# The FFN norm's variance kept spread over the features, the Newton step of queries and keys on GpSimd, and another slot order

## What is computed

```python
# attention, 16 heads of 64, windows of 32 tokens with one window of look-back
q, k, v = split(shift_tokens(x) @ Wqkv)
q = l2norm(q) * qs;  k = l2norm(k) * ksc      # then rotary tables
x = softmax(q k^T * 8, masked) v @ Wo + x
# gated FFN, inner width 341
t = shift_tokens(x)
mu = t.mean(-1);  var = ((t - mu) ** 2).mean(-1)
xn = (t - mu) / sqrt(var + 1e-5) * g + bln
a, gate = split(xn @ W1 + b1)
x = (a * gelu(gate)) @ W2 + b2 + x
```

## Time and profile before

| | |
|---|---|
| median of 3 runs | 3552.26 us |
| profiled execution, its own time | 3551.83 us |
| its span | 3550.0 us |
| TensorE busy, weight loads | 97%, 74% |
| VectorE busy | 91% |
| ScalarE busy | 77% |
| GpSimd busy | 73% |
| DMA queues | 18% of 16 engines |

### The profile page before, as it was taken

One profiled execution on the slowest core, in us unless ns is written; L12 is line 12 of the kernel. 1 busy time (PEld: TensorE's weight loads), 2 busy tenths in 40 slices (PEclk: granted clock), 3 DMA queues, 4 the chain that ended last, 5 costly groups with the idle time before them and its releaser, 6 DMA issues.

```text
span 3550.0 us, 112382 instructions
## 1 busy us (share of the span) xinstructions
PE 3451.3 (97%) x44743; PEld 2622.1 (74%) x45216; DVE 3216.1 (91%) x5485; ACT 2734.4 (77%) x4727; POOL 2583.4 (73%) x2267
## 2 busy tenths in 40 slices
PE   8998899999999999999999999999999999999998
PEld 6775577777777777777777777777777777777776
DVE  6876999999999999999999999999999999999995
ACT  5665687787887788788788778778878878877876
POOL 3334878777778777777877877877877877777772
PEclk9999999999999999999999999999999999999999
DMA  1001212212212212211221221221221221122121
GB/s 47 24 2 46 49 42 57 57 44 55 54 37 57 66 38 52 54 48 46 66 50 39 54 57 38 66 51 40 53 57 44 60 51 47 39 75 51 35 51 41
DMA packets 61717, 171.67 MB, mean 48 GB/s; under 512 B 9488, under 2 KB 21264, under 8 KB 60816
## 3 DMA queue, kind: packets, MB, share of 16 engines
q1 hardware_dynamic: 61200, 164.46, 18.1%
HBM read 21.82 MB, written 4.19 MB: 7 GB/s over the span
## 4 chain that ended last, share of the span: by engine, by line
PE 95%; issue 2%; ACT 1%; DVE 1%; POOL 1%; DVEq 0%; POOLq 0%; ACTq 0%
PE bank L1017 11%; PE bank L998 10%; PE bank L959 10%; PE bank L1033 9%; PE bank L911 9%; PE bank L1366 8%; PE bank L982 7%; PE bank L912 7%; PE bank L910 5%; PE bank L1379 4%; PE bank L976 3%; PE bank L379 2%; PE bank L359 2%; PE bank L344 2%; PE bank L1334 1%
## 5 line engine op out<-in xcount | busy, mean ns | idle before, releaser
L1273 POOL TENSOR_TENSOR rotbuf<-mbuf 128x512 f32<-128x512 f32 x768 | 969.3, 1273 | 511.2 <-PE bank L959 322.6
L1287 POOL TENSOR_TENSOR rotbuf<-rotbuf,rs 128x512 f32<-128x512 f32 x768 | 786.7, 1045 | 66.2 <-DVE rs L1203 66.2
L1137 DVE TENSOR_REDUCE ss<-sq 128x8 f32<-128x512 f32 x768 | 516.1, 677 | 156.5 <-ACT sq L1059 156.4
L1297 POOL TENSOR_TENSOR probs<-probs,rden 128x768 f32<-128x768 f32 x384 | 564.5, 1470 | 121.4 <-DVE rden L1239 121.4
L1156 DVE TENSOR_TENSOR mbuf<-bank,table 128x512 f32<-128x512 f32 x768 | 527.9, 687 | 13.4
L1157 DVE TENSOR_TENSOR mbuf<-bank,table 128x512 f32<-128x512 f32 x768 | 522.1, 680 | 0.0
L1059 ACT ACTIVATE sq<-bank 128x512 f32<-128x512 f32 x768 | 457.8, 596 | 55.5 <-PE bank L912 22.6
L1017 PEld LDWEIGHTS bank<-probs_t,vbuf 96*64 96x64 f32 x12288 | 390.2, 138 | 144.4 <-issue 104.3
L1079 ACT ACTIVATE kbuf<-bank 128x512 f32<-128x512 f32 x384 | 217.4, 591 | 347.7 <-PE bank L959 347.7
L911 PE MATMUL bank<-weights,inputs 128*128 128x512 bf16 x1152 | 439.5, 382 | 36.8 <-issue 14.4
L959 PE MATMUL bank<-ident,rotbuf 128*128 128x128 f32 x3072 | 451.7, 275 | 13.8 <-DVE mbuf L1157 7.6
(11 more groups left out here) (112 smaller groups left out, 6056.7 us busy)
## 6 DMA issues: line engine op xcount, KB each, us to landing
vbuf<-v_stage SPq DMA_DIRECT2D x192, 384.0 KB, 4.4
vbuf<-v_stage SPq DMA_DIRECT2D x192, 256.0 KB, 4.0
vbuf<-v_stage SPq DMA_DIRECT2D x96, 128.0 KB, 4.5
stage<-in_wqkv SPq DMA_DIRECT2D x36, 256.0 KB, 5.1
weights<-in_wo SPq DMA_DIRECT2D x6, 512.0 KB, 6.6
out_t<-weights SPq DMA_DIRECT2D x1, 2048.0 KB, 6.3
weights<-out_t SPq DMA_DIRECT2D x1, 2048.0 KB, 9.8
out_t<-weights SPq DMA_DIRECT2D x16, 128.0 KB, 2.3
```

The costliest lines, as they stand in the source:

```text
L1137: e.tensor_reduce(b.ss[:, col:col + 8], b.sq[:, u % 2, :].rearrange("p (h d) -> p h d", h=8), AX_X, ALU.add).then_inc(s.sq_summed, 1)
L1273: e.tensor_tensor(b.rot[:, u, :], b.m1[:, u % 2, :], b.m2[:, u % 2, :], ALU.add).then_inc(s.rotated, 1)
L1287: e.tensor_tensor(v, v, r, ALU.mult).then_inc(s.scaled, 1)
L1297: e.tensor_tensor(probs, probs, b.rden[:, p % 2, :].unsqueeze(2).broadcast_to([P, 8, BLOCK_K]), ALU.mult).then_inc(s.probs, 1)
```

## The change

1. The variance is one product with the full 128 by 128 matrix of 1/128 as the stationary operand and the 256 columns of squares moving, as the mean is. So every partition (feature) holds the variance of every token, and nothing has to be brought back: `pe_ff_rstd`, its ring user `rb`, `dve_ff_variance` and `NORM_LAG` are gone.
2. The root is taken on 128 by 256 elements: `act_ff_seed` (Ln from PSUM, Exp, Square, on ScalarE), `dve_ff_refine` (two instructions on VectorE), and `dve_ff_norm` reads `ff_xc` and `ff_w`, both in SBUF, where it read PSUM. The bank of `mu` is free once the first of the two has read it (`ff_weighed`).
3. The Newton step of queries and keys, now 64 columns, is four instructions on GpSimd (`pool_refine`) in place of three on VectorE.
4. The ring has 26 users for 27, so a user's bank now turns from slot to slot (`work_bank` takes the instance), and the lists of TensorE, ScalarE, VectorE and GpSimd are in another order. In TensorE's list one more projection (`pj` 5) is done two instances ahead, and part of the attention's work of an instance lies one slot later.

```diff
-    for t in range(2):
-        mm = e.matmul(work_bank(b, "mu", 0)[:, N_TOK + t:N_TOK + t + 1], b.ff_sq[:, P * t:P * (t + 1)], b.inv_dim[:, 0:1],
-                      start=True, stop=True)
-    mm.then_inc(s.ff_variance, 1)
-
-
-def pe_ff_rstd(e, s, b, at, ahead):
...
+    e.matmul(work_bank(b, k, "mu", 0)[:, N_TOK:2 * N_TOK], b.inv_dim[:, :], b.ff_sq[:, :], start=True, stop=True).then_inc(s.ff_variance, 1)
...
+def act_ff_seed(e, s, b, at, ahead):
...
+    e.wait_ge(s.ff_variance, k.c[1] + 1)
+    e.wait_ge(s.ff_normed, k.c[1])
+    w = b.ff_w[:, :]
+    e.activation(w, work_bank(b, k, "mu", 0)[:, N_TOK:2 * N_TOK], ACT.Ln, bias=b.ff_consts[:, 0:1]).then_inc(s.ff_logged, 1)
+    e.wait_ge(s.ff_logged, k.c[1] + 1)
+    e.activation(w, w, ACT.Exp, bias=b.ff_consts[:, 1:2], scale=-0.5).then_inc(s.ff_seeded, 1)
...
-def dve_refine(e, s, b, at, ahead):
...
+def pool_refine(e, s, b, at, ahead):
...
     e.tensor_tensor(a, y, y, ALU.mult).then_inc(s.newton, 1)
     e.wait_ge(s.newton, k.c[REFINE_OPS] + 1)
-    e.scalar_tensor_tensor(a, a, -0.5, x, ALU.mult, ALU.mult).then_inc(s.newton, 1)
+    e.tensor_tensor(a, a, x, ALU.mult).then_inc(s.newton, 1)
     e.wait_ge(s.newton, k.c[REFINE_OPS] + 2)
-    e.scalar_tensor_tensor(y, a, 1.5, y, ALU.add, ALU.mult).then_inc(s.newton, 1)
+    e.tensor_scalar(a, a, -0.5, 1.5, ALU.mult, ALU.add).then_inc(s.newton, 1)
+    e.wait_ge(s.newton, k.c[REFINE_OPS] + 3)
+    e.tensor_tensor(y, y, a, ALU.mult).then_inc(s.newton, 1)
...
+    w, a = b.ff_w[:, :], b.ff_sq[:, :]
+    e.wait_ge(s.ff_squared, k.c[1] + 1)
+    e.scalar_tensor_tensor(a, work_bank(b, k, "mu", 0)[:, N_TOK:2 * N_TOK], LN_EPS, a, ALU.add, ALU.mult).then_inc(s.ff_weighed, 1)
+    e.wait_ge(s.ff_weighed, k.c[1] + 1)
+    e.scalar_tensor_tensor(w, a, 3.0, w, ALU.subtract, ALU.mult).then_inc(s.ff_rooted, 1)
...
+    e.wait_ge(s.ff_rooted, k.c[1] + 1)
+    x = b.ff_xc[:, k.par, :]
+    e.scalar_tensor_tensor(x, x, -1.0, b.ff_w[:, :], ALU.mult, ALU.mult).then_inc(s.ff_normed, 1)
```

More of the change, by code:

```diff
@@ L818, in dve_deep_credit @@
     e.sem_inc(s.ff_centred, FIRST_N)
-    e.sem_inc(s.ff_var_kept, FIRST_N)
+    e.sem_inc(s.ff_weighed, FIRST_N)
+    e.sem_inc(s.ff_rooted, FIRST_N)
     e.sem_inc(s.ff_normed, FIRST_N)
@@ L892, in pe_wait_bank @@
             elif user == "mu":
-                e.wait_ge(s.ff_var_kept, c[1] + 1)
-            elif user == "rb":
-                e.wait_ge(s.ff_normed, c[1] + 1)
+                e.wait_ge(s.ff_weighed, c[1] + 1)
             elif user == "up":
@@ L900, in pe_wait_bank, with work_bank @@
             return
-def work_bank(b, kind, i):
-    return b.work[ring_place(kind, i) % WORK_BANKS]
+def work_bank(b, k, kind, i):
+    j = ring_place(kind, i)
+    return b.work[(len(WORK_RING) * (k.m - WORK_RING[j][2]) + j) % WORK_BANKS]
 def three_products(e, out, x_parts, w_parts):
@@ L1030, in pe_project_out @@
         e.wait_ge(s.wo_loaded, 16 * (k.layer + 1))
-    out = work_bank(b, "out", 0)[:, 0:N_TOK]
+    out = work_bank(b, k, "out", 0)[:, 0:N_TOK]
     for chunk in range(INNER // P):
@@ L1161, in dve_clamp @@
 def dve_clamp(e, s, b, at, ahead):
-    k, ff = at(ahead), at(ahead - NORM_LAG)
-    if not (k.ok or ff.ok):
+    k = at(ahead)
+    if not k.ok:
         return
[L1167 to L1170, removed]
+    e.wait_ge(s.sq_summed, k.c[8] + 8)
     e.wait_ge(s.newton, k.c[REFINE_OPS])
@@ L1182, in act_seed @@
     e.activation(b.na[:, :], b.nx[:, :], ACT.Ln).then_inc(s.logged, 1)
[L1183 to L1186, removed]
+    e.wait_ge(s.scaled, k.c[8])
     e.wait_ge(s.logged, k.c[1] + 1)
     e.activation(b.rs[:, :], b.na[:, :], ACT.Exp, scale=-0.5).then_inc(s.seeded, 1)
-def dve_refine(e, s, b, at, ahead):
-    k, ff = at(ahead), at(ahead - NORM_LAG)
-    if not (k.ok or ff.ok):
+def pool_refine(e, s, b, at, ahead):
+    k = at(ahead)
+    if not k.ok:
         return
@@ L1402, in act_ff_square @@
     e.wait_ge(s.ff_centred, k.c[1] + 1)
-    e.wait_ge(s.ff_variance, k.c[1])
+    e.wait_ge(s.ff_rooted, k.c[1])
     e.activation(b.ff_sq[:, :], b.ff_xc[:, k.par, :], ACT.Square).then_inc(s.ff_squares, 1)
+def act_ff_seed(e, s, b, at, ahead):
+    k = at(ahead)
+    if not k.ok:
+        return
+    e.wait_ge(s.ff_variance, k.c[1] + 1)
[4 more added lines that the diff above has]
+    e.activation(w, w, ACT.Exp, bias=b.ff_consts[:, 1:2], scale=-0.5).then_inc(s.ff_seeded, 1)
+    e.wait_ge(s.ff_seeded, k.c[1] + 1)
+    e.activation(b.ff_sq[:, :], w, ACT.Square, scale=2.0).then_inc(s.ff_squared, 1)
 def act_ff_affine(e, s, b, at, ahead):
@@ L1657, in act_deep_slot @@
     act_ff_gelu(e, s, b, at, -3, 2)
+    act_square(e, s, b, at, 1, 6)
+    act_copy_t(e, s, b, at, 0, 5)
+    act_exp_of(e, s, b, at, -1, 3)
+    act_copy_v(e, s, b, at, 1, 0)
+    act_copy_t(e, s, b, at, 0, 6)
+    act_square(e, s, b, at, 1, 7)
+    act_copy_out(e, s, b, at, -1, 1)
+    act_ff_square(e, s, b, at, -2)
+    act_copy_pt_of(e, s, b, at, -1, 2)
+    act_seed(e, s, b, at, 1)
+    act_ff_seed(e, s, b, at, -2)
+    act_square(e, s, b, at, 2, 0)
+    act_copy_pt_of(e, s, b, at, -1, 3)
```

238 lines of the change are left out of this document (109 added, 129 removed), and 8 rows, old and new, of the table WORK_RING.

## The result

The changed kernel takes **3611.11 us** (median of four runs, 3609.51 to 3611.60), the kernel before 3554.41 in the same comparison: a ratio of 1.0161, 95% interval 1.0145 to 1.0177. It is slower by 57 us where 60 us less was forecast. The profiled execution took 3611.15 us, span 3609.3.

The account below looks back on a forecast made before the run. TensorE was taken to bound the 33.00 us slot; -0.48 work and -0.15 order gave 32.37. 91 x 0.63 = 57 us plus 2 to 3 for half-filled slots made -60: 3492 us, stated range 3455 to 3540.

Parts of the forecast that it names:

- TensorE's work: TensorE's slot: spreading product removed, variance costing about as before, 0.47 us; net -0.48 us, bounds -0.52 and -0.42.
- the four new passages: TensorE's order: three entries to scores after values, one to values after scores; each costs 0 to 0.1 us.
- That TensorE keeps the bound: Slot of 32.37 us: TensorE stays the limit, by 0.7 us over VectorE's 31.7.
- none or 0.3: TensorE's order: real waits for a bank, 0.2 us a slot before, would be none or 0.3 us.
- cost nothing in throughput; TensorE's longer list covers it: ScalarE: three more instructions, +1.2 to 1.4 us a slot, 27.8 of 32.4, without lengthening the slot.
- 1.6 us to spare: VectorE, before added waits for GpSimd: needs 30.7 us in a slot of 32.4.
- The waits for GpSimd: VectorE's L1454 and norm L1465, reading two SBUF operands, wait 0.5 us each, 1.0 for both; TensorE still bounds.
- Rival (a): VectorE takes over in part, through GpSimd meetings or order: slot 32.6 to 32.95, 3515 to 3547 us; chance 0.18.
- Rival (b): L1454 and L1465 wait out GpSimd's longest instruction every slot: 33.25 us, 3575; chance 0.11 with (c)'s worse end.
- Rival (c): Variance's bank held about 2.2 us; late engines lose 0.6 us a slot: 3550; chance 0.05 at about no change.
- the same: Newton step on GpSimd: latency from guess to scaled queries unchanged, 1.6 us before, about 1.2 plus three waits after.

Follow-up runs that it names:

- one swap: The changed kernel with square of projection 6 put ahead of the third gelu and its table load on ScalarE: 3534.14 us.
- three edits: The changed kernel with the FFN root's guess in PSUM, the clamp on ScalarE and the FFN's norm on GpSimd: 3551.15 us.
- the run with gate 3 later: The changed kernel with square 6 ahead of gelu 3, root's guess in PSUM, norm on GpSimd, and the third gate behind rotary products 6: 3550.25 us.

## Why the prediction was wrong

**TensorE's work: right, and more than forecast.** The spreading product went, the variance cost 0.43, and the four new passages paid nothing beyond what leaving a group costs anyway, the lower end of the bounds: 31.8 us without waits, where I had a slot of 32.37.

**That TensorE keeps the bound, and that the new order has real waits of "none or 0.3": this is the step that failed.** TensorE waited for banks 1.8 us in the slot: 31.8 + 1.8 = 33.6. What should have covered the others, "cost nothing in throughput; TensorE's longer list covers it" for ScalarE and "1.6 us to spare" for VectorE, compared sums per engine with the slot. ScalarE was to have 5 us to spare and has 5.9 (33.60 - 27.74), but not between projection 4 and square 6, where 9.2 us stand in a row on the loop. Its three new instructions (1613.13 to 1614.60) are not among them; what fills them is the gelus with copies between and the two table loads. The same holds for VectorE: its idle 1.43 us lie at one place, and 18.94 us of work without a gap lie in the loop. In a program whose order is fixed and whose ring has three banks, spare time is a matter of place. I had laid out no loop from engine to engine.

**The waits for GpSimd: right in kind, mis-sized in sum, and wrong in what they cost.** I took 1.0 us for L1454 and L1465 and found 0.71 + 0.51 = 1.2; I overlooked the clamp, 0.5 more. Their sum of 1.7 just fills the room that I counted for VectorE (32.37 - 30.7), so by my reckoning it cost next to nothing. Rival (a), at 0.18, came closest in mechanism, with gaps before transposes that name the rotary product, as the text had said; its price, 32.6 to 32.95, was short by 0.7. Its time of up to 3547 us would still have been a gain. Rival (b), the slower one, asked for 2.3 us of waits in a full VectorE. There were 1.7, in one that was not full. Rival (c) did not come in this order: after the variance TensorE has no wait for the bank; it came in the old one. (Its "free 0.11 us after the product" is the length of the copy alone; the bank was free at 1617.85, 0.7 us after the product's end.)

**GpSimd: right in the change.** The four instructions take 0.29 + 0.32 + 0.24 + 0.32 = 1.2 us, and from the guess to the first scaling behind them it is 2.0 us (1612.92 to 1614.90), as long as before. In the old order, with the Newton step alone, it was 0.8 us longer: all four stand there behind the probabilities, where VectorE had two short ones left, and the prediction's "the same" did not count the place.

```profile
1612.66 0.26 ACT L1190 ACTIVATE rs<-newton_a 128x64 f32<-128x64 f32 x1
...
1614.90 3.23 POOL L1291 TENSOR_TENSOR rotbuf<-rotbuf,rs 128x512 f32<-128x512 f32 x3
```

## What to carry to other kernels

Where engines follow fixed lists, don't ask only whether an engine's sum fits in the period. Follow one wait back from engine to engine until the instruction recurs one period earlier: the lengths of the stretches must add up to less than the period, and a table load or a wait for another engine's instruction counts if it stands in one of them. A loop that is found tells what binds now; when it was shortened here, the next one came up after 0.6 us of 2.2. When an engine idles ahead of an instruction whose input was ready long before on a third engine, look at what stands ahead on the engine between; one swap there was worth more (77 us) than three edits that took 2.2 us a slot off VectorE (60 us).

## What the runs showed of the hardware that I had not expected

- A clamp of 128x64 from SBUF to SBUF, with one input, waits for GpSimd too: 0.67 us against 0.19 for 66 columns before, and 1.30 in the run with gate 3 later. In the slot above it ended 0.05 us after the 1.47 us instruction that GpSimd had begun at 1610.74. The moment is the difference, not the columns: the fastest of the changed kernel's 96 clamps took 0.20 us (shortest, median, longest, ns), and the old one took 0.52 once. The Trainium skill ("SBUF — State Buffer", Who interferes with whom) counts this kind of instruction among those that can take the port that GpSimd shares; the trace agrees.

```profile
L1177 DVE TENSOR_SCALAR newton_x<-ss x96: 196/671/875, 351.0 to 3527.7; 128x64 f32<-128x64 f32 x96
```

- Waits for GpSimd act as a cushion. A removed one of 0.71 us came back for half at the next such instruction (0.36), and 0.60 us of additional work ahead of one left 0.04 in the slot. The price of an instruction next to such a wait is not its length.
- VectorE gets in between two GpSimd instructions that follow each other at once: three scalings in a row took 3.23 us around L1454 where three took 3.04 in the kernel before (at 3472.07). Of the three it is the second, which began while L1454 was still running, that took 1.22 in place of 1.04.
